# Gated attention with a routed feed-forward layer: part of the score sums on TensorE, token shares on ScalarE, new instruction orders

## What is computed

```python
def attention(q, k, v):              # q = ln(x), k = v = context, each (tokens, 16, 8)
    scores = einsum('sqd,skd->sqk', q, k) / sqrt(8)
    scores = where(tril, scores, -1e18)
    return einsum('sqk,skd->sqd', softmax(scores), v)
x = x + tanh(g_xattn) * attention(ln(x), ctx, ctx)
y = ln(x)
logits = y @ router_w.T + bias
rw, sel = top_k(logits, 2);  cw = softmax(rw) spread over the 8 experts
moe    = sum over e of cw[e] * (silu(y @ w1[e]) * (y @ w3[e])) @ w2[e]
shared = (silu(y @ sw1) * (y @ sw3)) @ sw2
x = x + tanh(g_ffn) * (moe + shared)
```

## Time and profile before

| | before |
|---|---|
| median of 3 runs | 635.24 us |
| profiled execution, its own time | 631.01 us |
| its span | 628.9 us |
| TensorE busy | 502.4 us (80%) |
| VectorE busy | 507.4 us (81%) |
| GpSimd busy | 415.7 us (66%) |
| ScalarE busy | 334.2 us (53%) |
| mean granted TensorE clock | 0.935 of full |

### The profile page before, as it was taken

The page is one execution under the profiler, slowest core; times in us unless marked ns, Lnnn a source line. Parts: engine busy times, 40 slices in busy tenths (PEclk is TensorE's granted clock), DMA queues, the critical chain, the costliest instruction groups (busy, mean ns, idle before and its releaser), DMA issues.

```text
span 628.9 us, 13339 instructions
## 1 busy us (share of the span) xinstructions
PE 502.4 (80%) x3644; PEld 446.6 (71%) x3644; DVE 507.4 (81%) x1037; ACT 334.2 (53%) x950; POOL 415.7 (66%) x423
## 2 busy tenths in 40 slices
PE   0237087979898988998898979898889998999970
PEld 0025046857788787877797878878887887999960
DVE  3997999979988999899798969899989978442231
ACT  4216305673658456844675565846663654555430
POOL 2111803278637268788778886888778887878874
PEclk9977589988999999999799979999999989999995
DMA  7970535255837777698758865788678896699942
GB/s 235 215 137 1 167 81 188 92 167 123 260 98 209 178 237 151 181 231 232 167 143 225 207 178 158 229 191 215 171 225 184 232 228 185 148 259 273 329 134 86
DMA packets 114693, 115.50 MB, mean 184 GB/s; under 512 B 10680, under 2 KB 83392, under 8 KB 114624
## 3 DMA queue, kind: packets, MB, share of 16 engines
q1 hardware_dynamic: 67440, 81.87, 45.9%
q0 software_dynamic: 20848, 20.27, 16.7%
q10 hardware_dynamic: 26336, 12.52, 7.0%
HBM read 83.01 MB, written 30.30 MB: 180 GB/s over the span
## 4 chain that ended last, share of the span: by engine, by line
DVE 27%; POOL 26%; PE 26%; issue 12%; ACT 6%; DMA 2%; POOLq 0%; SPq 0%; ACTq 0%; DVEq 0%
PE ps_g L1145 9%; POOL rows_in L636 8%; PE ps_y L1172 6%; POOL xo L678 6%; DVE pv L777 6%; PE ps_g L1132 4%; ACT xn L973 3%; POOL pv L670 3%; DVE prod L745 3%; DVE sc L750 3%; DVE pv L785 3%; DVE eo L888 3%; PE ps_o L1088 2%; POOL rstd L595 2%; PE ps_o L1101 2%
## 5 line engine op out<-in xcount | busy, mean ns | idle before, releaser
L1145 PE MATMUL ps_g<-xrT,wq 128*128 128x128 f32 x1528 | 192.6, 280 | 3.1 <-ACT xrT L1019 2.6
L678 POOL DMA_INDIRECT xo<-rows_out,idx x104 | 170.5, 1639 | 32.2 <-issue 31.6
L1145 PEld LDWEIGHTS ps_g<-xrT,wq 128*128 128x128 f32 x1528 | 183.1, 196 | 4.8 <-ACT xrT L1019 3.5
L636 POOL DMA_INDIRECT rows_in<-xn,idx x128 | 136.5, 1067 | 40.8 <-issue 40.8
L1172 PE MATMUL ps_y<-w2s,eo 128*128 (+1 forms) x1020 | 140.0, 280 | 16.4 <-DVE eo L888 9.6
L1172 PEld LDWEIGHTS ps_y<-w2s,eo 128*128 128x128 f32 x1020 | 128.9, 193 | 32.9 <-issue 28.9
L888 DVE TENSOR_TENSOR eo<-sil,ps_g 128x512 f32<-128x512 f32 (+1 forms) x132 | 87.2, 661 | 61.8 <-ACT sil L1011 57.4
L1011 ACT ACTIVATE sil<-ps_g 128x512 f32<-128x512 f32 (+1 forms) x132 | 76.0, 581 | 108.5 <-PE ps_g L1145 81.7
L1088 PE MATMUL ps_o<-pv,ident 128*128 128x384 f32 (+10 forms) x328 | 88.3, 411 | 45.2 <-DVE pv L785 25.0
L777 DVE TENSOR_TENSOR pv<-ct,ex 128x512 f32<-128x512 f32 (+21 forms) x144 | 89.0, 651 | 17.1 <-ACT ex L984 15.9
L1088 PEld LDWEIGHTS ps_o<-pv,ident 128*128 128x128 f32 x328 | 51.0, 197 | 68.3 <-issue 50.3
(11 more groups left out here) (101 smaller groups left out, 479.8 us busy)
## 6 DMA issues: line engine op xcount, KB each, us to landing
wq<-wall SPq DMA_DIRECT2D x191, 256.0 KB, 3.7
rows_out<-yr ACTq DMA_DIRECT2D x91, 128.0 KB, 4.0
xr<-rows_in SPq DMA_DIRECT2D x41, 258.0 KB, 4.8
xt<-in_x SPq DMA_DIRECT2D x7, 512.0 KB, 4.0
ct<-in_ctx SPq DMA_DIRECT2D x7, 512.0 KB, 5.0
out<-xo SPq DMA_DIRECT2D x7, 512.0 KB, 5.3
xo<-x POOLq DMA_DIRECT2D x6, 512.0 KB
rows_in<-empty SPq DMA_DIRECT2D x2, 1483.5 KB, 20.6
```

What stands on the lines that cost most here:

```text
L636: pool.indirect_dma_start(rows_in[u % RI], bass.IndirectOffsetOnAxis(ap=idx[:, u % 3, k * TT + t:k * TT + t + 1], axis=0), xn2[:, c % XN, ...
L678: pool.indirect_dma_start(xo[:, c % XO, t], None, rows_out[u], bass.IndirectOffsetOnAxis(ap=idx[:, u % 3, at:at + 1], axis=0), compute_op= ...
L1145: last = nc.tensor.matmul(ps_g[n % 2][:, q // HC, q % HC, a * P:(a + 1) * P], wq[:, b % WR, q * P:(q + 1) * P], xrT[:, i % 3, a * P:(a + 1 ...
```

## The change

- `DOTTED`: in chunk 0 the diagonals 0, 2, ... 14 and in chunk 1 the diagonals 0, 1, 3, 4, 6, 7, 9, 10, 12, 13 are no longer reduced by VectorE. TensorE sums their eight features with eight matmuls by `ident` that read `prod` with a step of eight (`dot`, unit `qs`), into `ps_r`, and ScalarE copies the sums into `sc` (`scores`, unit `qe`). A dot waits for the copy of the dot before; the product that reuses a buffer waits for the dot of three diagonals before; `max` waits for the last copy.
- `ADDED`: chunk 1 adds only the diagonals 3 and 5, as chunk 0 does.
- `share` moves from VectorE to ScalarE.
- The two inputs of the value product `pv` change places.
- `sums` writes one dummy tile instead of two in turn, and each pass waits for all earlier ones. `total`, `neg` and `dev` become pairs for a second layer norm on ScalarE, which `SECOND = []` leaves unused.
- `URG`, `AHEAD`, `PHASES` (now 100, 470 and 570) and some durations of the planner are new, and so all orders.

```diff
+    SECOND = []
+    SUMS = [BYACT, SECOND]
...
-    ADDED = [[g for g in range(1, 12, 2)] if c > 0 else [3, 5] for c in range(CHUNKS)]
+    ADDED = [[g for g in range(1, 12, 2)] if c > 1 else [3, 5] for c in range(CHUNKS)]
...
+    DOTTED = [[g for g in range(0, NH, 2)] if c == 0 else [g for g in range(NH - 1) if g % 3 < 2] if c == 1 else [] for c in range(CHUNKS)]
+    DOTS = [(c, g) for c in range(CHUNKS) for g in DOTTED[c]]
...
-        AHEAD = {'sil': 0.4, 'eo': 0.1, 'upR': 0.2, 'inv2': 0.2, 'scatter': 2.5, 'down': 0.1, 'xo': 0.1, 'upS': 0.6, 'scores': 0.4, 'gather': 2.5, 'rows': 0.6, 'fetch': 2.5, 'chain': 0.6, 'sums': 2.5, 'plus': 1.2, 'inv1': 2.5, 'store': 0.8, 'sum': 0.4, 'ln1s': 0.1, 'ln1b': 1.6, 'yr': 2.5}
-
-        PHASES = (140.0, 480.0)
+        AHEAD = {'sil': 0.4, 'upR': 0.6, 'inv2': 2.5, 'scatter': 1.6, 'down': 0.2, 'xo': 2.5, 'upS': 0.2, 'scores': 0.4, 'gather': 0.8, 'rows': 0.2, 'fetch': 0.1, 'values': 0.2, 'chain': 0.2, 'sums': 0.2, 'inv1': 2.5, 'store': 1.6, 'sum': 0.4, 'ln1s': 0.6, 'xrT': 0.2, 'again': 0.2, 'yr': 0.6}
+
+        PHASES = (100.0, 470.0, 570.0)
...
-                        put("act", "ln1s", ("ln1s", c, k, q), .95, [(("load", c), 5.)] +
+                        put("act", "ln1s", ("ln1s", c, k, q), .97 + .2 * k, [(("load", c), 5.)] +
                             waits(("inv1", c - 2) if c > 1 else None, ("neg", c) if k else None))
                     if k == 0:
-                        put("act", "ln1s", ("neg", c), .35, [])
+                        put("act", "ln1s", ("neg", c), .25, [])
...
-                put("pool", "inv1", ("inv1", c), 2.7, waits(("ln1a", c), ("ln1b", c - 2, TILE[c - 2] // 2 - 1) if c > 1 else None))
+                put("pool", "inv1", ("inv1", c), 3.0, waits(("ln1a", c), ("ln1b", c - 2, TILE[c - 2] // 2 - 1) if c > 1 else None))
...
+                if g in DOTTED[c]:
+                    before = dots_to(c, g) - 2
+                    put("pe", "dots", ("qs", c, g), .24 + n * (NH - g) * HD * (.0025 if c == 0 else .00166),
+                        waits(("qk", c, g), ("qe", *DOTS[before]) if before >= 0 else None))
+                    put("act", "dots", ("qe", c, g), .2 + .001 * n * (NH - g),
+                        waits(("qs", c, g), ("sub", c - 1, 1) if c else None))
...
-                        need(dve, s["score"], NH * m + g - PR + 1)
+                        if NH * m + g >= PR:
+                            c0, g0 = divmod(NH * m + g - PR, NH)
+                            if (c0, g0) in DOTS:
+                                dve.wait_ge(s["qs"], dots_to(c0, g0))
+                            else:
+                                dve.wait_ge(s["score"], scores_to(c0, g0))
...
-                    if g > 0:
+                    if g > 0 and g - 1 not in DOTTED[m]:
...
-                    dve.wait_ge(s["score"], NH * (m + 1))
+                    dve.wait_ge(s["score"], scores_to(m, NH - 1))
+                    need(dve, s["qe"], dots_to(m, NH - 1))
...
-                    nc.vector.tensor_tensor(paired(diag(pv, PV, m, g), n), by_head(ch)[:, :, 0:NH - g, :],
+                    nc.vector.tensor_tensor(paired(diag(pv, PV, m, g), n),
                                             ex[:, 0:n, g:NH, g].unsqueeze(3).broadcast_to([P, n, NH - g, HD]),
-                                            ALU.mult).then_inc(s["pv"], 1)
+                                            by_head(ch)[:, :, 0:NH - g, :], ALU.mult).then_inc(s["pv"], 1)
...
-                        need(act, s["total"], past + t - 1)
-                        nc.scalar.activation(passing[:, 0, t % 2], xt[:, h, t], ACT.Copy, accum_out=total[:, t:t + 1])\
-                            .then_inc(s["total"], 1)
+                        need(act, s[f"total{w}"], past + t)
+                        nc.scalar.activation(passing[:, w, 0], src[:, h, t], ACT.Copy, accum_out=total[w][:, t:t + 1])\
+                            .then_inc(s[f"total{w}"], 1)
...
+                elif unit == "share":
...
+                    act.wait_ge(s["th"], c + 1)
+                    for k in range(K):
+                        nc.scalar.activation(xn2[:, c % XN, k, 0:TILE[c], D], dd[:, 1, 0:TILE[c]], ACT.Identity,
+                                             bias=half_tg[:, 1:2], scale=half_tg[:, k:k + 1]).then_inc(s["share"], 1)
...
+            def scores(c, g):
+                n = TILE[c]
+                if c == 0:
+                    act.wait_ge(s["route"], 1)
+
+                need(act, s["sub"], 2 * c)
+                act.wait_ge(s["qs"], dots_to(c, g))
+                nc.scalar.copy(sc[:, 0:n, g:NH, g], tiled(ps_r[:, 0:n * (NH - g)], n)).then_inc(s["qe"], 1)
...
+            def dot(c, g):
+                n = TILE[c]
+                pe.wait_ge(s["qk"], NH * c + g + 1)
+
+                need(pe, s["qe"], dots_to(c, g) - 1)
+                for d in range(HD):
+                    last = nc.tensor.matmul(ps_r[:, 0:n * (NH - g)], ident[:], paired(diag(prod, PR, c, g), n)[:, :, :, d],
+                                            start=(d == 0), stop=(d == HD - 1))
+                last.then_inc(s["qs"], 1)
```

More of the change, by code:

```diff
@@ L58, in tiles_to @@
         return sum(TILE[a] for a in range(c + 1) if a in some)
+    SECOND = []
     FIRST_HERE = [c for c in range(CHUNKS) if c not in BYACT]
+    SECOND_HERE = [c for c in range(CHUNKS) if c not in SECOND]
+    SUMS = [BYACT, SECOND]
+    SECOND_TOGETHER = [c for c in SECOND_HERE if c in TOGETHER]
     def together(w, c):
@@ L103, in planned @@
     def planned():
[L104 to L108, removed]
@@ L374, in gated_attention_moe @@
         vall = sb("vall", [P, T])
-        total = sb("total", [P, T])
-        neg = sb("neg", [P, T])
-        dev = sb("dev", [P, T])
+        total = [sb(f"total{w}", [P, T]) for w in range(2)]
+        neg = [sb(f"neg{w}", [P, T]) for w in range(2)]
+        dev = [sb(f"dev{w}", [P, T]) for w in range(2)]
         passing = sb("passing", [P, 2, 2, D])
@@ L436, in gated_attention_moe @@
         COUNT = ps_o[:, (T + TT) * E:(T + TT) * E + E]
-        names = ("small w wall total neg dev vsum cst ident0 ident gates tanh rwt rwtc fill0 fill1 in0 in1 ct0 ct1 stats0 stats1 mv0 mv1 inv rstd shift0 "
-                 "shift1 xn0 xn1 qk scatter_pause gather_pause score mx sub exp sum rs pv o att x1 add plus xnt xntc xnc logit "
+        names = ("small w wall total0 total1 neg0 neg1 dev0 dev1 vsum cst ident0 ident gates tanh rwt rwtc fill0 fill1 in0 in1 ct0 ct1 stats0 stats1 mv0 mv1 inv rstd shift0 "
+                 "shift1 xn0 xn1 qk scatter_pause gather_pause score qs qe mx sub exp sum rs pv o att x1 add plus xnt xntc xnc logit "
                  "route d th share mask rank pos posi tab sc0 sc1 gu sil eo y xt turned yev sh mix out halves").split()
@@ L961, in means @@
-            def means(c):
-                act.wait_ge(s["total"], sum(TILE[a] for a in range(c + 1) if a in BYACT))
-                need(act, s["shift0"], c)
-                nc.scalar.activation(neg[:, 0:TILE[c]], total[:, 0:TILE[c]], ACT.Copy, scale=-1.0 / D)\
-                    .then_inc(s["neg"], 1)
+                        if w:
+                            act.wait_ge(s["x1"], c + 1)
+                        else:
+                            act.wait_ge(s_in[h], 16 * (c // 2 + 1))
+                        need(act, s[f"neg{w}"], sum(a in SUMS[w] for a in range(c)))
@@ new lines, in sums @@
+                        need(act, s[f"total{w}"], past + t)
+                        nc.scalar.activation(passing[:, w, 0], src[:, h, t], ACT.Copy, accum_out=total[w][:, t:t + 1])\
+                            .then_inc(s[f"total{w}"], 1)
+                    else:
+                        act.wait_ge(s[f"neg{w}"], sum(a in SUMS[w] for a in range(c + 1)))
+                        need(act, s[f"shift{w}"], c)
+                        need(act, s[f"dev{w}"], past + t)
+                        nc.scalar.activation(passing[:, w, 1], src[:, h, t], ACT.Square, bias=neg[w][:, t:t + 1],
+                                             accum_out=dev[w][:, t:t + 1]).then_inc(s[f"dev{w}"], 1)
@@ L1115, in turn_rows @@
                 u, r, w = RPAIRS[i]
+                if i == 0:
+                    need(pe, s["qe"], len(DOTS))
                 need(pe, s["turned"], i)
```

124 lines of the change are left out of this document (72 added, 52 removed).

## The result

| | before | changed |
|---|---|---|
| median (4 runs each, same chip) | 636.38 us | 666.64 us |
| profiled execution | 631.01 us | 668.51 us |
| span | 628.9 us | 666.7 us |

The ratio is 1.0494 (95% interval 1.0435 to 1.0554): slower by 4.9%, where I had forecast 1% faster and a range up to 643 us. The two profiled executions lie 37.5 us apart, the medians 30.3. The profiled execution of before is none of the four and lies 5.4 us under their median, that of the changed kernel 1.9 us over its own. Every ratio in this document takes the fast runs alone, those within 1.5% of the fastest of their kernel; of the two kernels with the old orders 5 of 12 and 4 of 6 runs fall outside, of every other kernel at most 2.

What follows compares the result with a forecast made beforehand. VectorE was taken to bound until about 92 us, no engine to have much room in the middle, TensorE to bind at the end. Terms of -3.2 and -3.0 us took the median 635.24 to 629.0 us, range 619 to 643.

Steps and rivals of the forecast that it cites:

- Point 2: Chunk 0: eight score sums moved to TensorE, two slow dots and six fast, make `max` later by +2.2 us.
- "all slow" bound: Chunk 0's score sums: upper bound with every dot at half clock, +7.0 us.
- Point 3: Chunk 1: ten score sums on TensorE spare VectorE's reduces, -4.4 us, bounds -5.6 and 0.
- a rival (632 us): Chunk 1's dots over 64 columns: strided reads at twice the price cost 3.1 us more, 632 us; chance 0.08.
- Point 1: Start of chunk 0: the first product starts near 16.4 us, behind four squaring passes, costing +3.3 us.
- Point 4: Other VectorE work before 92 us: fewer adds in chunk 1 -2.7 us, `share` on ScalarE -0.4, traded inputs zero.
- Point 5: Chunk 0's shared up-products: dots before them may keep the clock up, -1.2 us, bounds -3 and 0.
- Point 6: Whole kernel: new urgencies and a fourth phase change all orders and shorten the later chunk periods, -3.0 us.
- Rival (a): First two chunks: slow dots, TensorE stays at half clock, +8.9 us, 644 us; chance 0.18.
- Rival (c): End of kernel: backlog of the dense part and GpSimd's gathers lose the start's gain, 635 us; chance 0.15.

Runs made afterwards that it cites:

- the two kernels with the old orders: Not listed by name; one is the changed kernel without dots, with early first product and the urgencies, AHEAD and phases of before: 0.9941, on another chip 0.9900.
- the contiguous kernel: The changed kernel with dots reading the same number of columns contiguously, so the scores are wrong sums: 1.0295 of before.
- Filled gaps: The changed kernel with four added identity matmuls behind each dot of chunk 0, keeping TensorE at work while ScalarE copies: 1.0523 of before.
- a warm start: The changed kernel with 26 added identity matmuls on TensorE before the first dot: 1.0478 of before.
- the two kernels without dots: The changed kernel with DOTTED empty: 1.0039 of before; the same with an early first product (two dummy tiles, ScalarE's pair taken earlier): 0.9986.

## Why the prediction was wrong

**Point 2, the dots of chunk 0: the step that failed is "eight matmuls with `ident`" priced by the logit row.** I read "x8 in 1.88 us" as eight calls. It was chunk 0's logit, four tiles, so four calls, each of which stands in the trace twice; the row of sixteen was a chunk of eight tiles. A float32 matmul is two matmul instructions and two weight loads. The rows had told it: the 328 matmuls of L1088 are twice the calls. Chunk 0 makes 14 (one for each diagonal that isn't added), the seven chunks of eight tiles 10 diagonals x 2 each, the last chunk 10, together 164. So every dot was priced at half. With the count right, the cycles as they were later measured (4.1 us slow, about 2.5 fast) and the clock as I took it (two slow dots, six fast), the stage would have been 0.6 + 2 x 4.1 + 6 x 2.5 = 23.8 us, +12.6 rather than +2.2.

**The second half of that miss is the clock.** I let the dots rise to full clock after two. All eight of chunk 0 ran at half: the trace has no record of the clock there, but a dot of 56 columns takes 3.63 us in chunk 0 and 3.64 in chunk 1, where the granted clock is 0.50, and 1.97 in the contiguous kernel at 1.00. TensorE was busy 28.8 of 33 us there. Filled gaps did not change it, and a warm start sped up one dot and part of the next. With the right count my "all slow" bound would have been 0.6 + 8 x 4.1 = 33.4 us for the stage; it took 33.2, that is +22.0.

**Point 3, chunk 1.** Same count, and the step of the reads. I had it as a rival (632 us). At full clock a stepped dot of 96 columns takes 3.02 us (dots in chunk 1 only) and a contiguous one of 96, 104 or 120 columns 2.0, about sixteen times a floor of 0.11. The page "SBUF — State Buffer" of the Trainium skill, under its note on SBUF cachelines, says that an access that crosses a 16-byte line pays a penalty. The runs agree. "Twice the price" was right; its sum was too small since it counted eight matmuls and not sixteen, and not the loss of clock. Expected -4.4, measured +8.4, of which the waits for `ps_r` in VectorE's last products and before `max` are the visible part. That removed reduces gain time in chunk 1 was right for a dot of the price I had given it: with half of the matmuls the stage is 3.2 us shorter than without dots.

**Point 1, the late start:** right. Forecast 16.4 us and four squaring passes ahead of the pair; measured 16.76 and four. The pitch of a pass with its wait is 0.49 and 0.61 us, not 0.44 and 0.53: the hop after an accumulator read is 0.09 to 0.11, not 0.04. That it reaches the end agrees with the 0.5% between the two kernels without dots, but their intervals overlap.

**Point 4:** the trade of inputs does nothing, 653 ns a product against 651. Adds and shares did leave VectorE, but chunk 1's value stage got 1.7 us longer: between `sub` and the exponentials ScalarE was given an `xo` copy and six squaring passes of chunk 2 (106.9 to 110.8 us), and VectorE waited 4.79 us for it. That is the new order, not the edits.

```profile
113.70 5.11 DVE L819 TENSOR_TENSOR pv<-ex,ct 128x1024 f32<-128x1024 f32 x5 [4.79 <-ACT ex L1019]
```

**Point 5, clock:** not borne out. The dots didn't keep the clock up; the granted clock is 0.50 from 73.6 to 94 us, and of the shared products between them the first eight ran at half clock again, in 3.73 us, and the other eight at full, in 1.97. VectorE waits 3.34 us for the first `eo`.

**Point 6, orders:** in the two traces chunks 1 to 7 went 2.8 us faster, and the end gave 2.2 back. That this is near the forecast of -3.0 is luck: no row priced the new orders, and runs of one kernel lie further apart than this. The experiments on other chips put the new urgencies 0.4% behind the old ones, within their intervals. So the term has no settled sign; it is small.

**Rival (a), slow dots, was the one that came,** at 0.18 and priced 644. It named the mechanism, but its price carried the halved count. The range ended at 643 because every bound of the dots was built on that one number. **Rival (c)** was wrong: in the two traces nothing of the early delay was absorbed, and by the medians at least 27.7 us of it came through.

## What to carry to other kernels

Before a row prices a new operation, tie its count to the calls in the code: instructions in the row, divided by calls, is a number to write down. A wrong unit moves the forecast and every bound together, so no rival protects against it. And work that moves from a busy engine to an idle one still has to be faster there than the time between the steps that wait for it: VectorE's reduce of 0.6 us became a round trip of 4.1 us, and the chain of the first chunks had no slack.

## What the runs showed of the hardware

- A float32 matmul stands in the trace as two matmuls and two weight loads; sixteen of 8 to 64 columns take 3.6 us at half clock, and sixteen of 32 to 56 columns 1.9 to 2.0 at full.
- Reading the moving operand with a step of eight floats costs 1.8 ns a column: in the changed kernel 0.233 us for 128 columns (half clock), 0.218 for 120 and 0.191 for 104 (full clock), taken from start to start within a dot. It shows once this exceeds the floor of 0.11 (full clock) or 0.21 us (half clock) for each matmul: contiguous matmuls of 32 to 120 columns all start 0.112 us apart, and the dots of chunk 0, of up to 64 columns, are as long with the step as without.
- TensorE can be busy without a gap for 41 us (the kernel with filled gaps) and stay at half rate. The granted clock of the views does not show it: it reads 1.00 for 17 to 50 us in the changed kernel while the weight loads last 0.333 us each (0.192 at full rate). The trace holds no record of the clock ahead of 58.0 us in the changed kernel (65.3 with filled gaps), the first one is a rise to full, and a stretch without a record reads 1.00. There the durations of the weight loads are the surer reading.
